# A four-network GNN kernel: batch norms of network L2 from the accumulator, its blocks turned two ahead, and network L0's degree rows stored in three pieces

## What is computed

```
L0: h' = (1+eps)*h + A@h;  relu(h'@W1+b1)@W2+b2 -> relu -> log_softmax
L1: two GCN layers, A with self loops and D^-1/2 on both sides
L2: four layers, for i in range(4):
        z = (A@h + h);  z = relu(z @ W1[i] + b1[i]) @ W2[i] + b2[i]
        mean, var = over the 3125 nodes, per feature
        z = (z - mean) * rsqrt(var + 1e-5) * gamma[i] + beta[i]
        h = relu(z)
L3: two MixHop layers (powers 0, 1, 2 of the normalised A), batch norm between
```

## Time and profile before

| | us |
|---|---|
| median of 3 runs | 1222.59 (1221.93 to 1223.36) |
| the profiled execution's own time | 1222.72 |
| its span, first to last instruction | 1221.1 |
| TensorE busy (matmul) | 1134.4 |
| VectorE busy | 673.5 |
| ScalarE busy | 456.9 |

### The profile page before, as it was taken

How to read it: one execution, slowest core, us unless ns; L and a number is a source line. 1 busy time by engine, 2 the same in 40 slices (tenths; PEclk the granted TensorE clock), 3 DMA queues, 4 the chain that set the end, 5 groups by cost and what they waited for, 6 DMA issues and landing times.

```text
span 1221.1 us, 19323 instructions
## 1 busy us (share of the span) xinstructions
PE 1134.4 (93%) x6308; PEld 659.9 (54%) x6308; DVE 673.5 (55%) x2154; ACT 456.9 (37%) x1347; POOL 11.4 (1%) x37
## 2 busy tenths in 40 slices
PE   3778999999999999999898998997799999999997
PEld 3556667665554554545445545545455556554644
DVE  7999999995562335455355345365544325632311
ACT  4549988886672122201311312203422114811100
POOL 1000000000000000000000000000100000000000
PEclk9998799999999999999899899999899999999998
DMA  2100000001001013434124133299922213510001
GB/s 76 23 1 2 2 2 10 1 1 45 10 11 26 15 43 75 93 76 93 33 58 89 27 77 70 67 261 193 209 62 68 79 51 93 132 33 26 13 24 30
DMA packets 208150, 70.32 MB, mean 58 GB/s; under 512 B 180944, under 2 KB 207126, under 8 KB 208048
## 3 DMA queue, kind: packets, MB, share of 16 engines
q1 hardware_dynamic: 124672, 42.31, 15.5%
q10 hardware_dynamic: 83008, 25.39, 9.3%
q0 software_dynamic: 368, 1.34, 0.6%
HBM read 20.71 MB, written 28.26 MB: 40 GB/s over the span
## 4 chain that ended last, share of the span: by engine, by line
PE 81%; DVE 9%; DMA 4%; ACT 2%; issue 2%; SPq 1%; ACTq 0%; DVEq 0%; POOL 0%; POOLq 0%
PE PS L1181 51%; PE PS L890 8%; DVE HPb L754 4%; PE PS L2582 4%; PE PS L879 2%; PE PS L1548 2%; PE PS L855 2%; PE PS L2051 2%; PE PS L2057 2%; DVE HPb L705 2%; DMA di_d<-SM 1%; PE PS L1666 1%; PE PS L2089 1%; DMA Zf<-di_d 1%; PE PS L1226 1%
## 5 line engine op out<-in xcount | busy, mean ns | idle before, releaser
L1181 PE MATMUL PS<-ADJ,HPb 125*128 125x500 bf16 (+2 forms) x2250 | 450.9, 356 | 0.3
L1181 PEld LDWEIGHTS PS<-ADJ,HPb 125*128 125x128 f16 x2250 | 219.6, 98 | 225.2 <-issue 34.5
L926 ACT CAST ADJ<-PS 126x72 f32 (+7 forms) x784 | 193.2, 315 | 54.4 <-PE PS L890 18.9
L1181 PE MATMUL PS<-ADJ,Zf 125*128 125x500 bf16 (+2 forms) x1050 | 202.1, 352 | 0.0
L890 PE MATMUL PS<-HPb 128*128 128x150 bf16 (+3 forms) x784 | 195.7, 354 | 1.7 <-ACT ADJ L926 1.5
L1181 PEld LDWEIGHTS PS<-ADJ,Zf 125*128 125x128 f16 x1050 | 102.3, 97 | 93.9 <-issue 1.3
L754 DVE TENSOR_SCALAR HPb<-XRf,Zf 128x176 bf16<-128x176 f16 (+2 forms) x588 | 136.7, 294 | 1.8 <-PE PS L890 1.0
L879 PEld LDWEIGHTS PS<-HPb 128*128 128x128 bf16 x642 | 87.2, 143 | 63.9 <-issue 37.9
L879 PE MATMUL PS<-HPb 128*128 128x25 bf16 x642 | 92.2, 217 | 12.7 <-DVE HPb L754 11.9
L1850 DVE CUSTOM_DVE_ANT_0 HPb<-ADJ,HPb 125x625 bf16<-125x625 bf16 x125 | 101.2, 810 | 3.7
L1952 DVE TENSOR_SCALAR Zf<-PS,B_L 128x500 f32<-128x500 f32 (+2 forms) x28 | 19.1, 683 | 138.7 <-PE PS L2057 138.7
(11 more groups left out here) (333 smaller groups left out, 1061.7 us busy)
## 6 DMA issues: line engine op xcount, KB each, us to landing
adj_d<-ADJ ACTq DMA_DIRECT2D x25, 700.0 KB
HPb<-y_d SPq DMA_DIRECT2D x19, 187.5 KB, 2.8
HPb<-di_d SPq DMA_DIRECT2D x10, 250.0 KB, 3.4
adj_d<-ADJ ACTq DMA_DIRECT2D x25, 81.2 KB
ADJ<-in_x SPq DMA_DIRECT2D x1, 1562.5 KB
q_d<-HPb SPq DMA_DIRECT2D x25, 62.5 KB
HPb<-di_d SPq DMA_DIRECT2D x5, 305.2 KB
HPb<-s_d ACTq DMA_DIRECT2D x5, 250.0 KB, 3.7
```

Source lines behind the costliest of these rows:

```text
L926: e.copy(to, WPS[group % BANKS][0:PD, t0 * RESTS[q]:t1 * RESTS[q]] .rearrange("p (t d) -> p t d", t=t1 - t0)).then_inc(s_mv, 1)
L1181: mm = e.matmul(accs[q], H[0:PN, t, q, 0:P], cols, start=(t == 0 and (two or q == 0)), stop=(t == NT - 1 and (two or q == 1)), skip_group_ ...
```

## The change

1. **Degrees, L0.** The second store, formerly of spans 2 to 6, is split: at `c == 1` only span 2's rows are stored, now ahead of the loads of `x`, and at `c == 2` those of spans 3 to 6, after span 2's rows are loaded and ahead of `di_out(1)`. The last span's rows are loaded into another buffer (`DT6`) once all sums of L0 are done, not once span 5's degrees are.
2. **Statistics, L2.** They read the accumulator, without the bias. The bias is added to the joined mean instead. For the last span the copy to `Zf` stands behind scale and shift; for the others behind the span's own statistics.
3. **Blocks, L2.** Blocks 0 and 1 are turned into banks 6 and 7 (one each), block 2 into banks 4 and 5. TensorE turns all three before the next sum starts, and from then on keeps two blocks ahead. Block 2's scale, shift and relu are two VectorE instructions in place of one on ScalarE.
4. A semaphore of the build is merged into another one (`s_sc[1]`), and the numbers behind it move by one.

```diff
@@ SyncE, L0 @@
                     e.wait_ge(s_dt, k)
-                    done(E0["dg"], DG * c)
-                    e.dma_start(DT[0:NT, 0:nt * PN], deg_d[:, cols]).then_inc(s_dt, 16)
+                    if c == NC - 1 and not general:
+                        done(E0["agg"], NC)
+                    else:
+                        done(E0["dg"], DG * c)
+                    e.dma_start(degrees_at(c)[0:NT, 0:nt * PN], deg_d[:, cols]).then_inc(s_dt, 16)
...
                     if c == 1:
+                        third = slice((j0 + nt) * PN, (j0 + nt + SPANS[2][1]) * PN)
+                        rest = slice((j0 + nt + SPANS[2][1]) * PN, N)
+                        e.dma_start(deg_d[:, third].rearrange("(o t) d -> o t d", o=1), ADJ[PN:PD, :, third])\
+                         .then_inc(s_dt, 16)
                         for v, j, n in ((XRf[:, 8 * P:], 8, 7),
...
-                        rest = slice((j0 + nt) * PN, N)
+                    if c == 2:
                         e.dma_start(deg_d[:, rest].rearrange("(o t) d -> o t d", o=1), ADJ[PN:PD, :, rest])\
                          .then_inc(s_dt, 16)
@@ VectorE, L2 @@
+                    def results(c):
+                        e.tensor_scalar(span(Zf, c), first_of(P2, c), bias2(Q_B2, l), None, ALU.add)\
+                         .then_inc(E2["z"], 1)
...
                         done(E2["d2"], n)
-                        e.tensor_scalar(span(Zf, c), first_of(P2, c), bias2(Q_B2, l), None, ALU.add)\
-                         .then_inc(E2["z"], 1)
-                        done(E2["z"], n)
-                        line(e.bn_stats(STATS[:, 0, c, :], span(Zf, c)))
-                        row_sums(l, c)
-                        hop_weights(l, c)
+                        line(e.bn_stats(STATS[:, 0, c, :], first_of(P2, c)))
+                        line.sync()
+                        if c == NC - 1:
...
+                            line(e.bn_aggr(BNM, STATS[:, 0, 0:NC, :].rearrange("p t c -> p (t c)")))
+                            line.sync()
+                            e.sem_inc(s_bn["var"], 1)
+                        else:
+                            results(c)
+                            row_sums(l, c)
+                            hop_weights(l, c)
+                    line(e.tensor_tensor(BNM[:, 0:1], BNM[:, 0:1], bias2(Q_B2, l), ALU.add))
...
                     e.sem_inc(s_bn["ab"], 1)
+                    results(NC - 1)
+                    done(E2["z"], base + NC)
                     if last:
                         third_norm()
                     else:
+                        j, k = BLOCKS[2]
+                        zb = Zf[:, j * PN:(j + k) * PN]
+                        line(e.tensor_scalar(zb, zb, BNA[:, 0:1], BNB[:, 0:1], ALU.mult, ALU.add))
+                        line.sync()
+                        e.tensor_scalar(zb, zb, 0.0, None, ALU.max).then_inc(s_bn["rel2"], 1)
                         for b in range(NBL):
                             low_part("L2", b, l * NBL + b + 1, turned_block(b))
@@ ScalarE, L2, layers 0 to 2 @@
+                        relu(0)
+                        relu(1)
+                        for b in range(NBL):
                             e.wait_ge(s_bn["tr"], l * NBL + b + 1)
                             high_part("L2", b, turned_block(b))
+                            if 1 <= b <= NBL - 3:
+                                relu(b + 2)
@@ TensorE, L2 @@
-                        turn_block(l, 0)
+                        for b in range(3):
+                            turn_block(l, b)
                         sum_span(l + 1, 0, next_span(l))
...
                     if t in starts:
-                        if starts[t] + 1 < NBL:
-                            turn_block(l, starts[t] + 1)
                         done(E2["hp"], l * NBL + starts[t] + 1)
+                        if 1 <= starts[t] <= NBL - 3:
+                            turn_block(l, starts[t] + 2)
```

More of the change, by code:

```diff
@@ L269, in build @@
         DT = HPf[:, NT * FW + 4 * P:NT * FW + 6 * P].bitcast(BF16)
+        DT6 = XRf[:, 5 * P:6 * P].bitcast(BF16)
         GZ = HPf[:, NT * FW:NT * FW + 5 * P]
@@ L305, in build @@
         s_rowt, s_rowc = sem("s_rowt"), sem("s_rowc")
-        s_frow, s_fsum = (sem("s_f%d" % k) for k in range(2))
+        s_frow = sem("s_f0")
         s_flag, s_flag2 = sem("s_flag"), sem("s_flag2")
@@ L326, in build @@
         s_soft, s_sc = sem("s_soft"), [sem(f"s_sc{m}") for m in range(3)]
-        s_bn = {n: sem("bn_" + n) for n in ("var", "sd", "ab", "rel", "tr", "w")}
+        s_bn = {n: sem("bn_" + n) for n in ("var", "sd", "ab", "rel", "rel2", "tr", "w")}
         s_wt = sem("s_wt")
@@ L1240, in layers, with degrees_at @@
             DG = 2 if general else 1
+            def degrees_at(c):
+                return DT6 if c == NC - 1 and not general else DT
             def degree_landed(c, p):
-                return 16 * (2 + p + DG * c + (c if c > 1 else 0))
+                return 16 * (2 + p + DG * c + (c if c > 1 else 0) + (c > 2))
             if general:
@@ L1513, in degrees @@
                         for k, j in enumerate(tiles_of(c)):
-                            mm = e.matmul(DEGP[0:PN, j:j + 1], DT[0:NT, k * PN:(k + 1) * PN], ONEB[0:NT], start=(p + k == 0),
+                            mm = e.matmul(DEGP[0:PN, j:j + 1], degrees_at(c)[0:NT, k * PN:(k + 1) * PN], ONEB[0:NT], start=(p + k == 0),
                                           stop=(p == DG - 1), skip_group_check=True)
@@ L1817, in turned_block @@
             def turned_block(b):
+                if b < 2:
+                    return PS[0:PN, 6 + b, 0:BLOCKS[b][1] * P].rearrange("p (t f) -> p t f", f=P)
                 return RB[b % 2][0:PN, 0:BLOCKS[b][1] * P].rearrange("p (t f) -> p t f", f=P)
@@ L1999, in relu @@
                         j, n = blocks_of(l)[b]
+                        if j + n == NT:
+                            done(E2["z"], base + NC)
                         zb = Zf[:, j * PN:(j + n) * PN]
                         e.activation(zb, zb, ACT.Relu, bias=BNB[:, 0:1], scale=BNA[:, 0:1]).then_inc(s_bn["rel"], 1)
-                    relu(0)
-                    for b in range(len(blocks_of(l))):
-                        if b + 1 < len(blocks_of(l)):
-                            relu(b + 1)
-                        if not last:
+                    if last:
+                        for b in range(NB):
+                            relu(b)
+                    else:
+                        relu(0)
+                        relu(1)
+                        for b in range(NBL):
                             e.wait_ge(s_bn["tr"], l * NBL + b + 1)
                             high_part("L2", b, turned_block(b))
+                            if 1 <= b <= NBL - 3:
+                                relu(b + 2)
                     if last:
@@ L2079, in rest_of_layer, with turn_block, turn_last @@
                 e.sem_inc(s_bn["w"], 1)
-            def turn_block(l, b, ring=RB):
-                e.wait_ge(s_bn["rel"], l * NBL + b + 1)
-                if b >= len(ring):
-                    done(E2["hp"], l * NBL + b + 1 - len(ring))
-                j, n = blocks_of(l)[b]
-                for m in range(n):
-                    c = (j + m) * PN
-                    mm = e.transpose(ring[b % len(ring)][0:PN, m * P:(m + 1) * P], Zf[:, c:c + PN], IDF[:, :])
+            def turn_block(l, b):
+                if b == 2:
+                    e.wait_ge(s_bn["rel2"], l + 1)
+                else:
+                    e.wait_ge(s_bn["rel"], l * NB + (b + 1 if b < 2 else b))
+                j, n = BLOCKS[b]
+                for m in range(n):
+                    mm = e.transpose(turned_block(b)[:, m, :], zc_of(j + m), IDF[:, :])
+                mm.then_inc(s_bn["tr"], 1)
+            def turn_last(b):
+                e.wait_ge(s_bn["rel"], (LAYERS - 1) * NB + b + 1)
+                if b >= len(RB3):
+                    done(E2["hp"], (LAYERS - 1) * NBL + b + 1 - len(RB3))
+                for m in range(BT):
+                    mm = e.transpose(RB3[b % len(RB3)][0:PN, m * P:(m + 1) * P], zc_of(b * BT + m), IDF[:, :])
                 mm.then_inc(s_bn["tr"], 1)
@@ L2174, in layers @@
                 for b in range(3):
-                    turn_block(LAYERS - 1, b, RB3)
+                    turn_last(b)
                 if general:
                     for b in range(3, NB):
-                        turn_block(LAYERS - 1, b, RB3)
+                        turn_last(b)
             bank4 = PS[:, 4, :].bitcast(BF16)
```

23 lines of the change are left out of this document (11 added, 12 removed).

## The result

The changed kernel takes 1214.58 us (median of 4 runs, 1213.76 to 1215.07); the kernel before took 1222.26 beside it (4 runs, 1220.00 to 1223.36). Ratio 0.9939, 95% interval 0.9922 to 0.9956: 7.5 us gained, 5.4 to 9.5. Two later sets gave 0.9929 and 0.9935. The sign was right, the size was not.

What follows compares the result with a forecast made beforehand. TensorE, busy 1134.4 of 1221.1 us, was taken as the bound, so only its waits and half clock could change. Gains of 1.4 (L0), 1.9 (three layer ends) and 0.1 (last layer) make 3.4: 1219.2 us, range 1217.1 to 1221.3.

Steps and rivals of the forecast that it cites:

- Last layer of L2: End of L2's fourth layer: 0.45 us shorter, but mostly hidden by L3's wait for `di_d` rows; 0.1 us gained.
- done sooner, they may run at full clock: L2's third layer end: block 2's turns, made before the sum, may escape half clock; 0.3 us in place of 0.13.
- one stretch fewer: Rival at L2's layer ends: one half-speed stretch of TensorE goes, saving 1.7 us more, 1217.5 us; chance 0.13.
- The stores' 1.4: L0, `degrees(2)`: span 2's rows come earlier, cutting 1.4 us of TensorE's 1.73 us wait, bounds 0.3 and 1.73.
- silent time of `di_out(0)`: L0: after its last packets the next load still waits 4.1 to 5.6 us; by the skill's 2 us the wait would go.
- wait moved to span 3: Rival in L0: the rest store delays `di_out(1)` and span 3's rows, 6.4 us lost, 1225.6 us; chance 0.04.
- the rest store's issue: L0, SyncE's queue: storing spans 3 to 6 with nothing queued ahead costs 0.72 us to issue.
- the last wait: L0, TensorE before the last degrees: the load still waits for `di_out(4)`, so the 1.48 us stay.
- The last copy left the chain: Each L2 layer end: VectorE's copy of the last span moves behind scale and shift, leaving 0.45 us gained.
- The instructions on 625 columns: L2, block 2: VectorE's two instructions take 0.52 us each, at most 0.87.
- nothing waited for block 2: L2 layer ends: VectorE has block 2 ready 1.6 us after scale and shift, TensorE wants it at about 2.2.
- 0.06 too much: L2 layer ends: statistics on PSUM were taken to cost 0.06 us more than the 0.42 on SBUF.

Runs made afterwards that it cites:

- first_three_ends: The kernel before with the change's L2 edits except the last layer's new statistics and late copy, degree stores as before; 2.9 us gained (1.6 to 4.4).
- stats_only: The kernel before with statistics from PSUM and the late copy of the last span in all four L2 layers, blocks and relus as before; 1.6 us gained.
- blocks_only: The kernel before with L2's blocks turned two ahead and the third block's relu on VectorE, statistics still from SBUF; 1.1 us gained (-0.6 to 2.7).
- early_s_after: The changed kernel with ScalarE sending for L3's first row of `s_d` one block earlier; 9.2 us (7.4 to 11.2) below the kernel before.

## Why the prediction was wrong

**The step that failed** is "Last layer of L2": "L3's first product waits for rows of `di_d` ... I take 0.1, bounds 0 and 0.45". The earlier trace rows names the longest wait of VectorE, and I took it for the one that binds. It is followed within 2 us by a wait for another row, and TensorE's 2.68 us of idle time by half clock. From the traces of the two kernels the start gives 2.4 us. As a start at 41.0 to 41.2 came in two of nine traces without both edits too, its mean is 7/9 of that, 1.9, an estimate from few traces, and more than the time of `first_three_ends` leaves room for. Why the row of `s_d` lands earlier with both edits (34.9 in the mean, without them 35.5) is not shown.

**The second miss is the clock at the three ends.** I had "done sooner, they may run at full clock, up to 0.5 better; I take 0.3", and one stretch fewer as a rival at 0.13. It went in every trace with both edits: 1.7 us. I had treated as chance what is decided by the two edits together, 0.44 us less idle time and ten turns in a row behind it. `stats_only` has the shorter idle time (3.26) with five turns and 17.1 us at half clock, `blocks_only` ten turns behind the longer one (3.70) and 17.1 too. Why neither alone does it is not shown; no run had other idle times than these two.

**Sum:** 1.6 for the stores, 1.65 for the ends, 0.4 for the blocks, 1.7 for the clock at the ends and 1.9 at L3's start make 7.2; measured 7.5 (5.4 to 9.5). The agreement is partly luck: the stores may be worth up to twice their 1.6, and L3's start less than its 1.9.

**What held, and what only seemed to.** The stores' 1.4 met the timed 1.6, but the sum behind it was a wait alone. The load was forecast for 312.4 to 313.9 and came at 313.02, in a trace whose graph build had ended 0.95 us early: on the forecast's own clock that is 313.97, and `degrees(2)` gained 1.06 of its wait, not 1.3 to 1.7 (0.67 was left, where I had said under 0.5). The mean over all traces, 2.6 to 1.3 us, is near the forecast. What I left out is the half clock behind that wait, gone in most traces with the edit; only on the chip of `early_s_after` did `degrees(2)` still wait 1.85 us and half clock follow. The Trainium skill's 2 us (DMA: Bandwidth & Descriptors, Anatomy of one DMA), which I had set beside the silent time of `di_out(0)`, is given there for transfers that GpSimd issues; these are SyncE's, and in the changed kernel too nothing moved from 309 us until the load went at 313.02. No wait moved to span 3, and the rest store's issue took 0.69, as costed. `DT6`, which I had at nothing, was in no run by itself; the last wait has the same range with it as without, and half clock came at that place in four of six traces with it and in all fourteen without, too few to tell. The last copy left the chain: 0.42 at the first end, 0.45 forecast. The instructions on 625 columns took 0.60 and 0.49, against 2 x 0.52, and nothing waited for block 2.

Statistics on PSUM took 0.425 us for 250 columns, where those on SBUF took 0.421, so I had 0.06 too much there. The end came out at 0.42 all the same, since two other steps grew: from the statistics' end to the first relu 1.75 us in place of 1.69, and TensorE's wait in front of the last `outputs` 0.74 in place of 0.67. The Trainium skill (VectorE: DVE Perf Modes, The TRN2 errata), which by its fixed costs would add an estimated 0.065, does not fit this instruction; the measurement decides.

## What to carry to other kernels

Where an engine waits long for one transfer, read on for the next two waits on the same chain before calling a shorter path covered: the one that binds is the last to end, here `s_d` and not `di_d`. And a wait of TensorE that is followed by half clock costs its length and some 1.7 us more for each stretch, so small cuts near that point pay in steps. Count the half-speed stretches in several traces of the kernel before: where the count never varied (17.1 us in every one here) one fewer can be put down to an edit, and where it varies, as at L3's start and behind `degrees(2)`, only the mean over several traces of both kernels can.

## What the runs showed of the hardware

- Behind TensorE's waits at L3's start the clock stayed at 2.4 GHz after 0.65, 1.33, 1.36, 1.53, 1.63, 1.71, 1.75, 1.78, 1.87 and 2.51 us, and fell to 1.2 after 1.93, 1.97, 2.05, 2.20, 2.39, 2.68 and 2.81. Behind `degrees(2)` it stayed after 0.67 to 1.73 us (seven traces), 2.06 and 3.33, and fell after 1.83 to 3.54 in the eleven others. The engine's idle time ahead of the fall decides mostly, not strictly. The Trainium skill (TensorE: Matmul & The Clock Gate, What's actually happening) says of a kernel's start that how many matmuls run at the low clock varies from run to run. Behind the three ends here only the place varied: which layer had one stretch and which two. The sum was the same 17.1 us in all eleven traces.
- Four of the six rows of `di_d` took a median of 11.2 us from issue to landing in the first profile and 8.0 in that of the changed kernel, though GpSimd begins to issue them 18.6 us behind the first turn in both (865.13 and 860.01). The slow kind (33.3 to 33.8 in the tables) came in three of twenty traces, all of kernels whose L2 and L3 were as before; what decides it stays open, and no run changed VectorE's code with its work left the same. A row of `s_d` (125 KB), asked for 1.5 us earlier in `early_s_after`, landed 4.3 us earlier.
- A 500-number `di_out`, issued in 0.25 to 0.48 us elsewhere, takes 6.05 to 6.89 us on the queue where it comes behind `x` (seven traces). The store of 2,125 columns in that place takes 6.39 to 7.30 (thirteen), and that of 1,625 with nothing ahead 0.69.
